# Windowed attention of the second block: scores made twice, mask added by a bf16 product, fp32r parts

## The reference, cut to what matters

```python
qkv = x @ qkv_w.T                       # (4, 1024, 768)
q, k, v = ...                           # (4, 16 heads, 1024, 16) each
q = q * cos + rotate_half(q) * sin
k = k * cos + rotate_half(k) * sin
mask = block_mask(S)                    # (blk | glob | slide) & (j <= i)
scores = jnp.einsum('bhqd,bhkd->bhqk', q, k) * scale
scores = jnp.where(mask[None, None], scores, jnp.finfo(scores.dtype).min)
attn = jax.nn.softmax(scores, axis=-1)
out = jnp.einsum('bhqk,bhkd->bhqd', attn, v)
out = jnp.transpose(out, (0, 2, 1, 3)).reshape(B, S, E)
return out @ out_w.T
```

## Time and profile before

| what | value |
|---|---|
| time, median of 3 runs | 3543.53 us (3539.63 to 3559.12) |
| time of the profiled execution | 3536.14 us |
| its span in the profile | 3534.2 us |
| mean granted clock of TensorE | 0.915 of full speed |
| TensorE matmul / weight load busy | 2898.2 us (82%) / 1813.4 us (51%) |
| VectorE / ScalarE / GpSimd busy | 2095.9 (59%) / 1689.6 (48%) / 1095.5 us (31%) |

### The profile page before, as it was taken

How to read it: one execution, slowest core, us unless ns; L and a number is a source line. 1 busy time by engine, 2 the same in 40 slices (tenths; PEclk the granted TensorE clock), 3 DMA queues, 4 the chain that set the end, 5 groups by cost and what they waited for, 6 DMA issues and landing times. The chain is left out here.

```text
span 3534.2 us, 59852 instructions
## 1 busy us (share of the span) xinstructions
PE 2898.2 (82%) x18120; PEld 1813.4 (51%) x18120; DVE 2095.9 (59%) x4691; ACT 1689.6 (48%) x3357; POOL 1095.5 (31%) x1891
## 2 busy tenths in 40 slices
PE   6599999999983599977953999958688888797869
PEld 3234443444441589964522889824355555544434
DVE  6577777777628544445566444346477777436852
ACT  4256766677731354431122544413366667354535
POOL 3344443444401254431011544324322222020112
PEclk9679999999996799988976999979899999898879
DMA  7612222222213244330031444322211111000001
GB/s 260 228 61 74 78 73 71 76 75 76 68 60 120 73 88 90 80 76 12 0 120 54 81 93 91 58 63 83 79 50 52 50 52 51 20 1 13 0 14 48
DMA packets 171006, 248.63 MB, mean 70 GB/s; under 512 B 29752, under 2 KB 114104, under 8 KB 170832
## 3 DMA queue, kind: packets, MB, share of 16 engines
q1 hardware_dynamic: 138064, 211.81, 18.0%
q0 software_dynamic: 32768, 34.64, 6.1%
HBM read 152.94 MB, written 92.27 MB: 69 GB/s over the span
## 5 line engine op out<-in xcount | busy, mean ns | idle before, releaser
L1916 DVE CUSTOM_DVE_ANT_0 s0Ah_SD<-s0Ah_ps_s,s0Ah_table 128x1024 f32<-128x1024 f32 x512 | 607.2, 1222 | 210.7 <-PE s0Ah_ps_s L1971 164.1
L1940 ACT ACTIVATE s0Ah_PM<-s0Ah_ps_x 128x512 f32<-128x512 f32 x1024 | 533.7, 600 | 233.3 <-PE s0Ah_ps_x L1996 127.7
L1971 PE MATMUL s0Ah_ps_s<-s0Ah_plus_k,s0Ah_plus_q 48*128 48x512 f32 x1024 | 424.5, 479 | 67.4 <-DVE s0Ah_mx L1916 35.3
L1896 POOL TENSOR_TENSOR s0Ah_DG<-s0Ah_SD,s0Ah_mx 128x128 f32<-128x128 f32 x512 | 203.3, 404 | 469.4 <-DVE s0Ah_mx L1916 469.1
L1971 PEld LDWEIGHTS s0Ah_ps_s<-s0Ah_plus_k,s0Ah_plus_q 48*128 48x128 f32 x1024 | 168.1, 194 | 319.0 <-DVE s0Ah_mx L1916 214.4
L2182 ACT ACTIVATE s4Ch_PM<-s4Ch_SD,s4Ch_nb 128x260 f32<-128x260 f32 (+2 forms) x512 | 254.2, 497 | 146.0 <-POOL s4Ch_nb L2125 133.2
L2016 PE MATMUL s0Ah_ps_v<-s0Ah_PM,s0A_V 128*17 128x512 f32 x2048 | 273.6, 607 | 0.0
L2136 DVE CUSTOM_DVE_ANT_0 s4Ch_SD<-s4Ch_ps_s,s4Ch_table 128x260 f32<-128x260 f32 (+2 forms) x512 | 204.8, 407 | 77.7 <-PE s4Ch_ps_s L2227 62.1
L1996 PE MATMUL s0Ah_ps_x<-s0Ah_plus_q,s0Ah_plus_k 50*128 50x512 f32 (+3 forms) x640 | 238.3, 389 | 4.6 <-DMA s0Ah_minus_k<-s0A_parts 4.3
L2227 PE MATMUL s4Ch_ps_s<-s4Ch_ks,s4Ch_qs 96*128 96x256 bf16 (+2 forms) x896 | 141.5, 228 | 114.6 <-DVE s4Ch_mx L2136 58.8
L1996 PE MATMUL s0Ah_ps_x<-s0Ah_minus_q,s0Ah_minus_k 50*128 50x512 f32 (+3 forms) x640 | 219.0, 390 | 0.0
...
## 6 DMA issues: line engine op xcount, KB each, us to landing
...
```

The costliest lines, as they stand in the source:

```text
L1896: nc.gpsimd.tensor_tensor(DG[p % 3][:, r * TB + t, :], SD[i % NSD][:, t * P:(t + 1) * P], mx[p % 3][:, r * TB + t:r * TB + t + 1].to_broad ...
L1916: nc.vector.tensor_tensor_reduce(SD[i % NSD][:, :], ps_s[i % 2][:, :, :].rearrange("p a n -> p (a n)"), table[:, (TB - 1 - t) * P:(TB - 1 ...
L1940: nc.scalar.activation(PM[n % NPB][:, :], ps_x[u % NX][:, :], ACT.Exp).then_inc(e_ok, 1)
L1971: x = nc.tensor.matmul(ps_s[i % 2][:, half, :], q[at(r), t * P:(t + 1) * P], k[at(r), half * GT:(half + 1) * GT], start=True, stop=True)
```

## The change

The windowed attention takes the form of the first block's. `project_rotary` splits q and k into two fp32r parts each with a new class `SplitKeys`, built on `SplitSets`: q's rest is made on VectorE, k's on GpSimd. In HBM a row of k has for each of the 8 tiles 4 + 128 keys (KBLK = 132): the tile's own 128 and before them the 4 global keys, so that a score of a tile is one product of 264 columns. The programs are written out instead of looped; on VectorE the moments of the layer norm come first, and the subtraction of the group before stands behind the first products.

`heads_window` is new. SP issues five tables, five sets of loads (one pair each, a ring of NST = 5), ten DMAs of ones, two for v's global rows, and then, for each pair, the set five pairs ahead and the store of the pair before. VectorE has only the maxima left (and some memsets), GpSimd splits the maxima, issues their four row DMAs per pair, and copies the 4 global keys to KG. The maxima of a pair are wanted 2 pairs (LATE) ahead, and its first scores run 2.5 pairs (AHEAD) ahead. The mask of the second scores is put into the bank first, by a product of an identity with a table of 0 and a large negative number, both in bf16 (`hidden`), and the scores are added to it (`shifted`): keys of a tile against its own and the next 128 queries. The 4 global keys have products of their own (`global_scores`), for queries from the third tile on. The products with v of a pair stand in the turn of the next pair. The output goes through HBM to `project_heads`; `project_out`, `Split`, `load_head` and `batch_turns` go.

In the diff, lines that are removed are left out where the functions above show them.

```diff
 def attention_window(nc, ph, X, ident, a):
-    parts = nc.dram_tensor(f"{ph.name}_parts", (2, PARTS, B * D, T), BF16, kind="Internal").ap()
-    V = ph.sb("V", [P, B, H, TB, HD + 1])
+    qparts = nc.dram_tensor(f"{ph.name}_qparts", (2, B * D, T), F32, kind="Internal").ap()
+    kparts = nc.dram_tensor(f"{ph.name}_kparts", (2, B * D, TB * KBLK), F32, kind="Internal").ap()
+    OD = nc.dram_tensor(f"{ph.name}_OD", (B * H // 2, P, GT), F32, kind="Internal").ap()
     with ExitStack() as own:
-        project_rotary(nc, Phase(nc, own, ph.name + "p"), X, ident, a, parts, V)
-    AO = ph.sb("AO", [P, B, TB, H, HD])
+        V = ph.sb("V", [P, B, H, TB, HD + 1])
+        with ExitStack() as first:
+            project_rotary(nc, Phase(nc, first, ph.name + "p"), X, ident, a, qparts, kparts, V)
+        heads_window(nc, Phase(nc, own, ph.name + "h"), ident, a, qparts, kparts, V, OD)
     with ExitStack() as own:
-        heads_window(nc, Phase(nc, own, ph.name + "h"), ident, a, parts, V, AO)
-    with ExitStack() as own:
-        project_out(nc, Phase(nc, own, ph.name + "o"), X, ident, a["out_wT"], AO)
+        project_heads(nc, Phase(nc, own, ph.name + "o"), X, ident, a["out_wT"], OD)
...
-class Split:
...
-def load_head(sp, parts, n, q, k, loaded):
...
-def batch_turns(eng, turn):
...
+NGL = 4
+KBLK = NGL + P
...
+class SplitKeys(SplitSets):
+    def __init__(self, ph, qparts, kparts):
+        super().__init__(ph, qparts, 2, 1)
...
+    def keys(self, sp, g, part, tile):
+        s, b, h = g % 2, g // 2, g % 2
+        for c in range(DC):
+            rows = self.kparts[part, b * D + c * P:b * D + (c + 1) * P, :].rearrange("p (t w) -> p t w", w=KBLK)
+            here = tile[:, c, :].bitcast(F32)
+            sp.dma_start(rows[:, h * G:(h + 1) * G, NGL:], here.rearrange("p (t q) -> p t q", q=P)
+                         ).then_inc(self.written[s], 16)
+            if h == 0:
+                sp.dma_start(rows[:, :, 0:NGL], here[:, 0:NGL].unsqueeze(1).to_broadcast([P, TB, NGL])
+                             ).then_inc(self.written[s], 16)
+    def sync(self, sp, g):
+        s, b, h = g % 2, g // 2, g % 2
+        to = lambda part: self.parts[part, b * D:(b + 1) * D, h * GT:(h + 1) * GT].rearrange("(c p) t -> p c t", p=P)
+        sp.wait_ge(self.top_ok, START + g * 2 + 1)
+        sp.dma_start(to(0), self.top[s][0][:, :, :].bitcast(F32)).then_inc(self.written[s], 16)
+        sp.wait_ge(self.rd_ok, START + g + 1)
+        sp.dma_start(to(1), self.rest[s][0][:, :, :].bitcast(F32)).then_inc(self.written[s], 16)
+        sp.wait_ge(self.top_ok, START + g * 2 + 2)
+        self.keys(sp, g, 0, self.top[s][1])
+        sp.wait_ge(self.rp_ok, START + g + 1)
+        self.keys(sp, g, 1, self.rest[s][1])
...
-    split = Split(ph, parts)
+    split = SplitKeys(ph, qparts, kparts)
...
+            for g in range(NG):
+                if g < NG - 2:
+                    ln.pool(pool, g + 2)
+                if g:
+                    split.pool(pool, g - 1, 1)
                 for s in range(2):
+                    split.before_f(pool, g, s)
                     pool.wait_ge(ab_ok, START + (2 * g + s + 1) * DC)
+                    nc.gpsimd.tensor_tensor(split.F[s][:, :, :], AB[:, s, 0, :, :], AB[:, s, 1, :, :],
...
+            for g in range(NG):
+                h = g % 2
                 now = lambda t: t[:, h * GT:(h + 1) * GT]
+                if g < NG - 2:
+                    ln.vector_moments(dve, g + 2)
                 for s in range(2):
                     dve.wait_ge(split.f_ok, START + 2 * g + s - 1)
                     for c in range(DC):
                         nc.vector.tensor_tensor(AB[:, s, 0, c, :], ps_q[:, c, :], now(cos), ALU.mult)
                         nc.vector.tensor_tensor(AB[:, s, 1, c, :], ps_r[:, c, :], now(sin), ALU.mult
                                                 ).then_inc(ab_ok, 1)
-                if more:
-                    ln.vector_moments(dve, g + 2)
-                if more:
+                    if s == 0 and g:
+                        split.vector(dve, g - 1, 0)
+                if g < NG - 2:
                     ln.vector_rows(dve, g + 2)
-                split.vector(dve, g, h)
-            batch_turns(dve, turn)
+            split.vector(dve, NG - 1, 0)
...
+def heads_window(nc, ph, ident, a, qparts, kparts, V, OD):
...
+    AHEAD = 2 * U + U // 2
+    NST, NS, NX = 5, 3, 4
+    WS = 2 * KBLK
+    LATE = 2
...
+            def load(p):
+                s = p % NST
+                q, k = Q[s][:, :].bitcast(F32), K[s][:, :].bitcast(F32)
+                for r in range(2):
+                    rows = slice((2 * p + r) * HD, (2 * p + r + 1) * HD)
+                    z = r * 64
+                    sp.dma_start(q[z:z + 2 * HD, :], qparts[0:1, rows, :].to_broadcast([2, HD, T])
+                                 ).then_inc(st_in[s], 16)
+                    sp.dma_start(q[z + 2 * HD:z + 3 * HD, :], qparts[1, rows, :]).then_inc(st_in[s], 16)
+                    sp.dma_start(k[z:z + 2 * HD, :], kparts[0:2, rows, :]).then_inc(st_in[s], 16)
+                    sp.dma_start(k[z + 2 * HD:z + 3 * HD, :], kparts[0, rows, :]).then_inc(st_in[s], 16)
+            def store(p):
...
+            sp.dma_start(near[:, :], masks[:, 0, 0:P]).then_inc(tabled, 16)
+            for n in range(2):
+                for k in range(2):
+                    sp.dma_start(table[:, n, k * KBLK + NGL:(k + 1) * KBLK], masks[:, n + 1, k * P:(k + 1) * P]
+                                 ).then_inc(tabled, 16)
+            for p in range(NST):
+                sp.wait_ge(zero_ok, START + p + 1)
+                load(p)
+            sp.wait_ge(ones_ok, START + 1)
+            for k in K:
+                for r in range(2):
+                    sp.dma_start(k[r * 64 + SROW:r * 64 + MROW, :].bitcast(F32), ones[:, :]).then_inc(oned, 16)
+            sp.wait_ge(clear_ok, START + 1)
+            for r in range(2):
+                heads = V[0:NGL, :, :, 0, :].rearrange("p b h d -> p (b h) d").rearrange(
+                    "p (n r) d -> p n r d", r=2)[:, :, r, :]
+                sp.dma_start(VG[r * NGL:(r + 1) * NGL, :, r, :], heads).then_inc(vg_in, 16)
+            for p in range(NP):
+                if p + NST < NP:
+                    sp.wait_ge(x_mm, START + last_use(p) + 1)
+                    load(p + NST)
+                if p >= 1:
+                    store(p - 1)
...
+            def maxima(p):
+                pool.wait_ge(e_ok, START + turn_use(p) + 1)
+                nc.gpsimd.tensor_tensor(NMp[p % 2][1][:, :], NM[:, :], NMp[p % 2][0][:, :].bitcast(F32),
+                                        ALU.subtract).then_inc(nr_ok, 1)
+                pool.wait_ge(nr_ok, START + p + 1)
+                for r in range(2):
+                    for n in range(2):
+                        z = r * 64 + SROW + n
+                        pool.dma_start(Q[p % NST][z:z + 1, :].bitcast(F32).rearrange("a (t q) -> a t q", t=TB),
+                                       NMp[p % 2][n][r * TB:(r + 1) * TB, :].bitcast(F32)).then_inc(rows_in[p % 2], 16)
+            for p in range(NP):
+                if p < LATE:
+                    maxima(p)
+                else:
+                    maxima(p)
+                    global_keys(p - 1)
+                if p == 0:
+                    global_keys(0)
...
+            for i in range(N):
+                p, t, r = i // U, i % U // 2, 1 - i % 2
+                n = WS if t else P
+                mask = near[:, :] if t == 0 else table[:, 1 if t >= 2 else 0, :]
                 dve.wait_ge(s_mm, START + i + 1)
+                nc.vector.tensor_tensor_reduce(SD[i % NS][:, 0:n], ps_s[i % NS][:, 0:n], mask, 1.0, -3e38, ALU.add, ALU.max,
+                                               accum_out=mx[p % 3][:, r * TB + t:r * TB + t + 1]).then_inc(m_ok, 1)
...
+            def exps(p, r, blk):
+                u = score_use(p, r, blk)
+                n = GT if blk < 3 else GT - P
+                act.wait_ge(x_mm, START + u + 1)
+                if p >= 2:
+                    act.wait_ge(pv_mm, START + p - 1)
+                nc.scalar.activation(PM[p % 2][:, 2 * blk + r, 0:n], ps_x[u % NX][:, 0:n], ACT.Exp, scale=HD ** -0.5
                                      ).then_inc(e_ok, 1)
...
+            for p in range(LATE):
+                negated(p)
+            for p in range(NP):
+                for blk in range(4):
+                    for r in range(2):
+                        exps(p, r, blk)
+                    if blk < 2:
+                        global_exps(p, blk)
+                    if blk == 2:
+                        if p + LATE < NP:
+                            negated(p + LATE)
+                        if p:
+                            collect(p - 1)
+            collect(NP - 1)
...
+            def score(i):
+                p, t, r = i // U, i % U // 2, 1 - i % 2
+                q, k = Q[p % NST], K[p % NST]
+                if i % U == 0:
```

(64 more changed lines are left out.)

511 lines of the change are left out of this document (167 added, 344 removed).

## The result

| | before | changed |
|---|---|---|
| median of the runs that stand beside each other | 3551.3 us | 3653.5 us |
| range | 3539.6 to 3566.3 | 3647.5 to 3660.8 |
| ratio, 95% interval | | 1.0293 [1.0254, 1.0332] |
| span of the profiled execution | 3534.2 us | 3659.0 us |
| mean granted clock of TensorE | 0.915 | 0.832 |

What follows compares the result with a forecast made beforehand. It took the loads to bound the new heads loop at 13.0 us per pair; heads and output -7 and projection -13.5 summed to -20.5 us, 3523 us on the median, range 3480 to 3572.

Steps and rivals of the forecast that it cites:

- the clock falls in the gaps: Heads loop: TensorE idles 3 us in 13 at late loads, pairs up to 17 us, 3635 us; chance 0.04.
- Two tiny copies: GpSimd, heads loop: counted with one small subtraction and four row DMAs at 3 us per pair in all.
- all three lie under TensorE's 9.9: Heads loop: VectorE 6.9, ScalarE under 6.8 and GpSimd 3 us per pair are hidden behind TensorE's 9.9 us.
- The likeliest case: Heads loop bound by its loads at about 13 us per pair, 3495 to 3548 us; chance 0.62.
- The load queue: SP loads in the heads loop: one set of eight loads per pair takes 12.3 us and bounds the loop.
- Start of the main loop: Heads part: tables, five load sets, ones and GpSimd's first rows put it 75 us after the heads start.
- The pace 13.0: Heads loop: 13.0 us per pair, from 12.3 for a load set and 0.7 for the store.
- the 0.7 for the store: Heads loop: the store of 0.26 MB adds 0.7 us per pair to the load queue.
- TensorE 9.9 us a pair: Heads loop: TensorE's products for one pair of heads sum to 9.9 us, below the loads' 13.0.
- Projection: Projection of the changed stage: -8 us from shorter waits and -5.5 us from the tail, sum -13.5 us.
- A group 19.2 us: Projection: a group that lasted 20.5 us would take 19.2 us, with TensorE waiting less for VectorE's products.
- Output: End of the stage: `project_heads` takes 58 us after the last collect, against 44.3 before the change.

Runs made afterwards that it cites:

- e1: Changed kernel with each mask product issued twice into its bank: 3545.1 us, ratio to before 0.9945.
- e8: Changed kernel with an added mask product per mask product, using 16 rows of its operands instead of 128: 3807 us (one run).
- e9: Changed kernel with GpSimd copying the previous pair's global keys ahead of the split and row DMAs: 3599 us, ratio to before 1.0164.
- e11: Changed kernel with 24 mask products once ahead of the main loop and the global-key copy ahead of the row DMAs: 3567 us (3505 to 3580).
- e3: Changed kernel without mask products and without v products but for the last key tile (wrong output): 3498.7 us (one run).
- e7: Changed kernel with 24 mask products ahead of the loop, loads as twelve DMAs of 16 rows, and the global-key copy ahead: 3417 us, ratio to before 0.9659.

## Why the prediction was wrong

- **What failed is the clock.** Every term of the loop behind pair 0 was priced at 2.4 GHz. I had the case as a rival (the clock falls in the gaps, up to 17 us a pair, 3635 us) with a chance of 0.04, on the row that TensorE with 80 of 100 us busy had 1.00. Size and pace of that rival were right (16.7 us, 3653), its chance was not. The row told of another mix of work, with transposes and stacked scores; e1 against e8 shows that the mix counts. What in the old loop kept its clock up, no run shows.
- **Its trigger was another one.** I had the gaps at late loads. At 1.2 GHz there are none; the loop starts cold at 2590.67, and each of its two rises ends in the wait for the copied global keys. "Two tiny copies" and "all three lie under TensorE's 9.9" is the step that failed on GpSimd: their 0.42 us is nothing, but they stand behind a subtraction and four issues and start 2.8 us after it does (2891.58 to 2894.39), and at 2.4 GHz TensorE is there first. Of a step that is cheap, its place in the queue has to be priced.
- **The likeliest case could not last.** A loop at full clock, bound by its loads with TensorE idle in each pair, is what e9 and e11 have for a few pairs, some 12.3 us apart, with waits of 0.6 to 2.2 us for K; after two to five of them the clock is gone for longer. In these two runs a bound of the loads turned into a bound of TensorE at half the clock for most of the loop.
- **The load queue.** 12.3 us a set: sets 2 and 3 land 12.0 and 12.6 us behind one another (2537.09, 2549.12, 2561.71). Start of the main loop 75 us: 73.7. The pace 13.0: e3 gave 12.3, the price of the set alone; the 0.7 for the store shows nowhere. With the clock up it would have been the bound, so this step was right but for that term.
- **TensorE 9.9 us a pair** at 2.4 GHz: 10.1 in e7, with no wait in it.
- **Projection.** A group 19.2 us: 19.1. Its sum -13.5: measured -9.8. The arithmetic ends sooner, at 2507.4 against 2513.8, but the stores, issued until 2509.1, hold the stage's end to 2516.94; before, heads followed 4 us behind. Only even groups store pieces of 16 bytes, so the last one has none. Those of the group before it are issued from 2494.4 to 2500.8, the last group's stores stand behind them, and the DMA engines are busy until about 2514:

```profile
2500.00:2520.00 20.00, 1.99 (x8) 1.44 (x8) 3.49 (x4) 2.81 (x5) 7.16 (x8) 0.64 0.89 133
```

  I had the pieces covered by two groups of 20 us; the last of them have 13 us of work left over them. No run leaves them out, so that they are the cause is argued from this window.
- **Output** 58 us: 57.6.

Heads part and output took 618 + 58 = 676 us, 136 above my 540, all of it in the loop; the profiled execution missed my sum by 124.8 + 20.5 = 145 us, and the rest is the 3.7 of the projection and 6 in unchanged stages.
